# One chunk more of lead for the turned and rectified rows in the second and third mean pass of a graph kernel

## The chip, the cores and the metric

The kernel runs on one core of a Trainium2 chip. The metric is the device time of one execution in microseconds (us); lower is better. Three timed executions of the kernel before stand beside one profiled execution.

## The reference

The inputs are 50,000 nodes with 128 features (`x`), 25,000 edges (`src`, `dst`, sorted by `dst`) and edge features. Two layers follow each other; the change lies in the first.

```python
def _sage_conv(x, src, dst, Wl, bl, Wr):
    msg = x[src]
    summed = jax.ops.segment_sum(msg, dst, num_segments=N_NODES)
    mean = summed / jnp.maximum(cnt, 1.0)[:, None]
    return mean @ Wl.T + bl + x @ Wr.T
h = jax.nn.relu(_sage_conv(x, ...Wl0, bl0, Wr0))
h = jax.nn.relu(_sage_conv(h, ...Wl1, bl1, Wr1))
h = _sage_conv(h, ...Wl2, bl2, Wr2)
x = _layernorm(x + h)      # then an edge attention and a second layernorm
```

## The kernel before

Edges are cut into 49 chunks of 512 (NC), nodes into 98 (NN). There are three mean passes, `mean0`, `mean1` and `mean2`, one for each convolution. Each walks over the 49 edge chunks, computes the segment sums as a running scan that a flag resets, and writes mean times Wl to a table in HBM (`mean_product`). `mean1` and `mean2` read the table of the pass before them, so a pass can gather only when all stores of the pass before have landed. Beside their 49 edge chunks, `mean1` and `mean2` also carry half of the node chunks each through a "dense" chain, which is what a node without incoming edges needs.

One step of `mean1` or `mean2` works on several chunks at once. `run(engine, phase, stages, count)` writes for each engine its stages in a fixed order, each with a lead: in step s a stage with lead k treats chunk s+k. Engines agree through semaphores alone. Before the change, step s holds, in this order on each engine:

- TensorE (PE): `mean_prod` s+1 (L894, four products of the scanned sums with Wl), `mean_turn` s+3 (L883 turns the gathered rows GX into bank5, L887 adds hsrc times Wr), then the dense chain: `chain_t` s+9 (L771), `chain_1` s+8 and `chain_2` s+7 (both L849), `chain_y` s+6 (L869).
- ScalarE (ACT): `mean_keep` s+3 (L1062, relu of bank5 into `hsrc`), dense `keep_t` s+9 (L1026), `keep_1` s+8 (L1031), `keep_2` s+7 (L1036), `inverse_root` s+6 (L1047, L1050), `bias_y` s+8 (L1040).
- VectorE (DVE): `mean_seg` s+3 (L1385, the scan of hsrc into `seg`), `mean_scale` s+1 (L1392, into `prod`), dense `add_x` s+6 (L1339, then L1347 and L1352, the statistics), `norm` s+5 (L1363).
- SyncE's DMA queue: the flags of chunk s+6 (L564), the dense rows XN of s+13 (L551), the store of mean_product s+1 (L569) and the store of the dense result s+5 (L558).
- GpSimd (POOL): four indirect gathers of 128 rows for each chunk into GX (L672), and a copy of indices every four chunks (L662). GX has 8 buffers; the gather of chunk c waits until `mean_turn` of chunk c-8 is done.

`mean_turn` waits for its gathered rows and, since bank5 is the only bank for it, for `mean_keep` of the chunk before. `mean_keep` waits for `mean_turn` of its chunk, and writes to a place in `hsrc` of its own for each chunk. `mean_seg` waits for `mean_keep` of its chunk, for its flags and for the scan before. `inverse_root` waits for the statistics that VectorE makes in the same step.

Of the kernel before, what the change touches and what calls it, by code (L numbers as in the profile page):

```python
# [37 lines left out]
DENSE = 5  # L38
# [87 lines left out]
def run(eng, phase, stages, count, to_end=True, middle=None):  # L126

    stages = [(*one, count)[:3] for one in stages]  # L130
    whole = min(chunks - 1 - lead for lead, _, chunks in stages) // U

    def single(s):
        for lead, f, chunks in stages:
            if 0 <= s + lead < chunks:
                f(At(phase, (s + lead) // U, (s + lead) % U, to_end and s + lead == chunks - 1))

    for s in range(-max(lead for lead, _, _ in stages), 0):
        single(s)
    if middle:  # L140
        middle()
    with eng.Fori(0, whole) as j:
        for u in range(U):
            for lead, f, _ in stages:
                f(At(phase, j, u + lead))
    for s in range(whole * U, count):
        single(s)
# [15 lines left out]
def gnn_kernel(nc, x, src, dst, ea, Wl0, bl0, Wr0, Wl1, bl1, Wr1, Wl2, bl2, Wr2,  # L163
# [27 lines left out]
    with ExitStack() as ctx:  # L191
# [577 lines left out]
        def _(pe):  # L769
# [156 lines left out]
            for i in range(3):  # L926
                if i == 0:
                    run(pe, "mean0", [(LAG + 1, mean_turn), (0, look_up), (LAG, mean_prod)], NC, middle=table_sums)
                    look_done.end(pe, "mean0")
                    for one in (6, 7):  # L930
                        pe.matmul(bank[one][:, :], ident[:, :], hsrc[:, 0:CH], start=True, stop=True).then_inc(y_cleared, 1)
                else:
                    dense = first if i == 1 else second
                    run(pe, f"mean{i}", [(1, mean_prod), (3, mean_turn), (DENSE + 4, dense(chain_t)), (DENSE + 3, dense(chain_1)),
                                         (DENSE + 2, dense(chain_2)), (DENSE + 1, dense(chain_y))], NC)
                m_h.end(pe, f"mean{i}")
            m_scaled.end(pe, "mean2")
# [70 lines left out]
        def _(act):  # L1008
# [55 lines left out]
            for i in range(3):  # L1064
                if i:
                    m_seg.end(act, f"mean{i - 1}")
                if i == 0:
                    run(act, "mean0", [(0, mean_keep)], NC)
                    act.wait_ge(y_cleared, 2)
                    act.wait_ge(small_loaded, 16 * (H + 3))  # L1070
                else:
                    dense = first if i == 1 else second
                    run(act, f"mean{i}", [(3, mean_keep), (DENSE + 4, dense(keep_t)), (DENSE + 3, dense(keep_1)),
                                          (DENSE + 2, dense(keep_2)), (DENSE + 1, dense(inverse_root)), (DENSE + 3, dense(bias_y))], NC)
            run(act, "dst", [(4, keep_t), (3, keep_1), (2, keep_2), (1, inverse_root), (3, bias_y)], NC)
            y_done.end(act, "dst")
# [497 lines left out]
```

## Time and profile before

| what | value |
|---|---|
| median of 3 runs | 2632.78 us (2631.59 to 2633.68) |
| profiled execution, its own time | 2643.03 us |
| its span | 2641.2 us |
| PE, DVE, ACT, POOL busy over the span | 68%, 65%, 43%, 67% |
| `mean1`, first to last scan | 463.9 to 750.9 us |
| `mean2`, first to last scan | 780.3 to 1066.6 us |
| all DMA traffic of the program | 357.05 MB, mean 135 GB/s |

The two passes together are some 600 us of the 2641. Busy shares are averages over stages with different limits, so they do not tell what sets the pace in these two passes; the views of the passes do.

### The profile page before, as it was taken

How to read it: one execution, taken by the hardware profiler on the slowest of the kernel's cores; microseconds unless marked ns; L12 is line 12 of the kernel's file. 1: busy time of each engine (PE TensorE's matmuls, PEld its weight loads, DVE VectorE, ACT ScalarE, POOL GpSimd, SP SyncE). 2: the span in 40 equal slices, each digit the busy share in tenths (PEclk: the TensorE clock that was granted, in tenths of full speed). 3: DMA queues.
4: the chain of work that ended last, by engine and by line, in shares of the span. 5: the costliest groups of instructions: out<-in, count | busy, mean ns of one | idle time of the engine just before them, and what ended most of it. 6: DMA issues, size and time to landing. Idle time of an engine off the chain costs nothing.

```text
span 2641.2 us, 42521 instructions
## 1 busy us (share of the span) xinstructions
PE 1787.9 (68%) x9906; PEld 1270.0 (48%) x9906; DVE 1719.1 (65%) x5656; ACT 1142.2 (43%) x2655; POOL 1778.3 (67%) x1895
## 2 busy tenths in 40 slices
PE   4755667988879889676777663888788788770000
PEld 2335665656656656455555453555555555540000
DVE  7777886878767778565555533888788788871000
ACT  7951112545445545132222222776666666640000
POOL 0047775676657666467777777777777777776776
PEclk7558989999999999788888885999999999985555
DMA  0025666899989998544444613455545445433321
GB/s 20 1 65 145 166 158 137 187 175 187 182 173 184 202 176 182 152 139 122 129 134 133 171 59 106 145 158 155 145 139 151 144 147 153 148 95 106 93 92 51
DMA packets 366865, 357.05 MB, mean 135 GB/s; under 512 B 46547, under 2 KB 288862, under 8 KB 366722
## 3 DMA queue, kind: packets, MB, share of 16 engines
q1 hardware_dynamic: 310274, 246.46, 30.9%
q0 software_dynamic: 56448, 109.10, 22.9%
q14 instruction: 105, 0.86, 0.1%
q8 instruction: 38, 0.62, 0.1%
HBM read 232.89 MB, written 129.11 MB: 137 GB/s over the span
## 4 chain that ended last, share of the span: by engine, by line
POOL 23%; issue 21%; DVE 20%; PE 15%; DMA 9%; ACT 8%; DVEq 1%; SPq 1%; POOLq 1%; ACTq 0%
POOL hsrc L672 9%; POOL GX L672 8%; POOL out_dram L726 4%; DVE stats L1347 4%; PE bank L849 4%; DMA GX<-in_x_dram,idx_a 2%; PE bank L923 2%; PE bank L771 2%; PE bank L853 2%; ACT normed L1017 2%; DVE prod L1392 2%; DMA XN<-in_x_dram 2%; ACT hsrc L1062 2%; ACT normed L1018 2%; DVE res L1339 2%
## 5 line engine op out<-in xcount | busy, mean ns | idle before, releaser
L672 POOL DMA_INDIRECT GX<-mean_product,idx_a x392 | 416.2, 1062 | 125.4 <-issue 113.8
L672 POOL DMA_INDIRECT GX<-in_x_dram,idx_a x392 | 378.9, 967 | 117.8 <-issue 109.1
L849 PE MATMUL bank<-h,wt 128*128 128x512 f32 x588 | 328.2, 670 | 1.2 <-ACT h L1036 0.9
L1047 ACT ACTIVATE logv<-mv,eps 128x4 f32<-128x4 f32 x245 | 72.3, 295 | 518.7 <-DVE mv L1352 518.6
L726 POOL DMA_INDIRECT x_prime<-normed,idx_b x196 | 198.5, 1013 | 88.0 <-issue 81.7
L726 POOL DMA_INDIRECT out_dram<-XN,idx_b x196 | 193.1, 985 | 74.7 <-issue 63.4
L672 POOL DMA_INDIRECT hsrc<-x_prime,idx_d x196 | 190.3, 971 | 59.7 <-issue 59.7
L672 POOL DMA_INDIRECT GX<-in_edge_attr_dram,idx_a x196 | 189.3, 966 | 58.6 <-issue 54.1
L672 POOL DMA_INDIRECT hsrc<-x_prime,idx_c x196 | 186.3, 951 | 59.7 <-issue 59.7
L1385 DVE TENSOR_TENSOR_SCAN seg<-flag,seg,hsrc 128x512 f32<-128x512 bf16 x98 | 126.1, 1286 | 115.5 <-ACT hsrc L1062 73.4
L869 PEld LDWEIGHTS bank<-wt,h 128*128 128x128 f32 x1176 | 153.0, 194 | 49.8 <-issue 47.4
L771 PE MATMUL bank<-ident,XN 128*128 128x128 f32 x784 | 131.4, 294 | 65.8 <-DMA XN<-in_x_dram 27.4
L771 PE MATMUL bank<-ident,hsrc 128*128 128x128 f32 x468 | 86.5, 316 | 124.2 <-DMA hsrc<-x_prime,idx_d 67.3
L894 PE MATMUL bank<-wt,seg 128*128 128x128 f32 x1176 | 163.0, 283 | 7.2 <-DVE prod L1392 4.8
L1142 ACT ACTIVATE normed<-bank,shift,rstd 128x128 f32<-128x128 f32 x392 | 147.7, 457 | 45.4 <-DVE shift L1542 45.2
L771 PE MATMUL bank<-ident,GX 128*128 128x128 f32 x392 | 73.1, 318 | 133.6 <-DMA GX<-in_x_dram,idx_a 133.6
L1334 DVE TENSOR_TENSOR res<-bank,GX 128x512 f32<-128x512 f32 x49 | 33.9, 691 | 196.5 <-PE bank L869 196.3
L1363 DVE TENSOR_SCALAR normed<-res,mv,rstd 128x128 f32<-128x128 f32 x588 | 161.5, 352 | 0.0
L853 PEld LDWEIGHTS bank<-ident,hsrc 128*128 128x128 f32 x784 | 127.7, 231 | 68.3 <-issue 68.3
L771 PEld LDWEIGHTS bank<-ident,XN 128*128 128x128 f32 x784 | 100.6, 151 | 123.9 <-issue 120.3
L869 PE MATMUL bank<-wt,h 128*128 128x128 f32 x1176 | 157.2, 277 | 0.8 <-ACT h L1036 0.8
L894 PEld LDWEIGHTS bank<-wt,seg 128*128 128x128 f32 x1176 | 148.8, 198 | 13.5 <-DVE seg L1385 12.8
(222 smaller groups left out, 4584.2 us busy)
## 6 DMA issues: line engine op xcount, KB each, us to landing
mean_product<-prod SPq DMA_DIRECT2D x147, 256.0 KB, 4.0
hsrc<-mean_product SPq DMA_DIRECT2D x147, 256.0 KB, 4.3
XN<-in_x_dram SPq DMA_DIRECT2D x98, 256.0 KB, 6.4
x_prime<-normed SPq DMA_DIRECT2D x98, 256.0 KB
XN<-x_prime SPq DMA_DIRECT2D x98, 256.0 KB, 4.5
out_dram<-normed SPq DMA_DIRECT2D x98, 256.0 KB
flag<-same_dst_row SPq DMA_DIRECT2D x147, 128.0 KB, 5.5
XN<-low_row SPq DMA_DIRECT2D x98, 128.0 KB
```

The source lines that it names most:

```text
L672: pool.indirect_dma_start(buf[:, c.slot(U), t, :], None, table, bass.IndirectOffsetOnAxis(ap=idx[:, c.slot(U), t:t + 1], axis=0)).then_inc ...
L726: pool.indirect_dma_start(table, bass.IndirectOffsetOnAxis(ap=idx_b[:, c.slot(U), t:t + 1], axis=0), rows[:, t, :], None, bounds_check=N - ...
L771: return pe.transpose(dst, src, ident[0:src.shape[0], 0:src.shape[0]])
L849: last = pe.matmul(psum[:, :], wt[:, T_R[i], :], before[:, c.slot(2), :], start=True, stop=not dst_phase)
L853: last = pe.matmul(psum[:, t * P:(t + 1) * P], PL[:, c.slot(U), i, t, :], ident[:, :], start=False, stop=t == TPC - 1)
L869: last = pe.matmul(y[:, t * P:(t + 1) * P], h2[:, c.slot(2), t * P:(t + 1) * P], wt[:, T_R[2], :], start=False, stop=t == TPC - 1, skip_gr ...
L894: last = pe.matmul(bank[3 + c.slot(2)][:, t * P:(t + 1) * P], seg[:, c.slot(2), t * P:(t + 1) * P], wt[:, T_L[int(c.phase[-1])], :], start ...
L1047: act.activation(logv[:, s, :], mv[:, s, :, 1], ACT.Ln, bias=eps[:, 0:1]).then_inc(n_log.of(c), 1)
L1142: last = act.activation(normed[:, node.slot(4), t, :], norm_rows(node)[:, t, :], ACT.Identity, bias=shift[:, s, t:t + 1], scale=rstd[:, s, ...
L1347: last = dve.bn_stats(stats[:, s, t, :], rows[:, t, :])
L1363: last = dve.tensor_scalar(normed[:, c.slot(4), t, :], norm_rows(c)[:, t, :], mv[:, s, t, 0:1], rstd[:, s, t:t + 1], ALU.subtract, ALU.mult)
L1385: dve.tensor_tensor_scan(seg[:, c.slot(2), :], flag[:, c.slot(4), :], rows, seg[:, before.slot(2), CH - 1:CH], ALU.mult, ALU.add).then_inc ...
```

## The change

The stages `mean_turn` on TensorE and `mean_keep` on ScalarE get lead 4 in place of 3 in `mean1` and `mean2`. The scan on VectorE keeps lead 3. No instruction is added or removed.

```diff
@@ -931,7 +931,7 @@
                 else:
                     dense = first if i == 1 else second
-                    run(pe, f"mean{i}", [(1, mean_prod), (3, mean_turn), (DENSE + 4, dense(chain_t)), (DENSE + 3, dense(chain_1)),
+                    run(pe, f"mean{i}", [(1, mean_prod), (4, mean_turn), (DENSE + 4, dense(chain_t)), (DENSE + 3, dense(chain_1)),
                                          (DENSE + 2, dense(chain_2)), (DENSE + 1, dense(chain_y))], NC)
@@ -1070,7 +1070,7 @@
                 else:
                     dense = first if i == 1 else second
-                    run(act, f"mean{i}", [(3, mean_keep), (DENSE + 4, dense(keep_t)), (DENSE + 3, dense(keep_1)),
+                    run(act, f"mean{i}", [(4, mean_keep), (DENSE + 4, dense(keep_t)), (DENSE + 3, dense(keep_1)),
                                           (DENSE + 2, dense(keep_2)), (DENSE + 1, dense(inverse_root)), (DENSE + 3, dense(bias_y))], NC)
```

VectorE's order of instructions is the same before and after. On TensorE, this is the head of `mean1`, where the dense chain (L771, L849, L869) runs alone before the first turn:

```order
 L849 MATMUL bank<-h,wt 128x512 x2
 L869 MATMUL bank<-wt,h 128x128 x4
+L883 MATMUL bank<-ident,GX 128x128 x4
+L887 MATMUL bank<-hsrc,wt 128x512
 L771 MATMUL bank<-ident,XN 128x128 x4
 L849 MATMUL bank<-h,wt 128x512 x2
```

The first turn (L883, L887) now stands one step of the dense chain earlier. On ScalarE, this is the same place, where `keep` of the first chunk (L1062) moves ahead of one more step of the dense copies:

```order
 L1050 ACTIVATE rstd<-logv 128x4
 L1040 ACTIVATE bank<-b 128x512
+L1062 ACTIVATE hsrc<-bank,bcol 128x512
 L1026 ACTIVATE h<-bank 128x512
 L1031 ACTIVATE h<-bank,bcol 128x512
```

Every later L1062 then stands where the one of the chunk before stood, so inside the loop the rows read alike and only the chunk number differs. At the end of a pass on TensorE, after the dense chain has ended, one pair of turn and product rows falls away from between the products (L894):

```order
 L887 MATMUL bank<-hsrc,wt 128x512
-L894 MATMUL bank<-wt,seg 128x128 x4
-L883 MATMUL bank<-ident,GX 128x128 x4
-L887 MATMUL bank<-hsrc,wt 128x512
-L894 MATMUL bank<-wt,seg 128x128 x8
+L894 MATMUL bank<-wt,seg 128x128 x12
```

The last turn has moved ahead by one step, and the last three products stand together.

## Rows read from the trace of the kernel before

**Rows 1.** Waits, 460 to 745 us (mean1): us in total, times, longest us.
```profile
POOL idx_a L662 <- PE bank L887: 40.3, 6, 14.2
...
DVE seg L1385 <- ACT hsrc L1062: 35.4, 40, 1.1
...
PE bank L883 <- ACT hsrc L1062: 16.3, 35, 1.8
...
PE bank L771 <- DMA XN<-in_x_dram: 15.3, 5, 7.0
DVE seg L1385 <- DMA flag<-same_dst_row: 12.2, 4, 4.2
```
**Rows 2.** Waits, 780 to 1060 us (mean2), same columns.
```profile
PE bank L883 <- ACT hsrc L1062: 17.8, 35, 1.8
```
**Rows 3.** Chain that ended last, one step of mean1: start us, us, what.
```profile
510.33 0.67 DVE prod L1392
511.00 0.61 DVE res L1339
511.63 0.88 DVE stats L1347 x4
...
512.82 0.23 DVE mv L1352 x2
...
513.07 0.31 ACT logv L1047
...
514.03 0.68 ACT hsrc L1062
```
**Rows 4.** Timeline, DVE, scans: start us, us, engine line op, [idle before <-releaser].
```profile
509.13 1.28 DVE L1385 TENSOR_TENSOR_SCAN seg<-flag,seg,hsrc 128x512 f32<-128x512 bf16 x1 [1.02 <-ACT hsrc L1062]
...
555.87 1.28 DVE L1385 TENSOR_TENSOR_SCAN seg<-flag,seg,hsrc 128x512 f32<-128x512 bf16 x1 [1.01 <-ACT hsrc L1062]
...
740.59 1.28 DVE L1385 TENSOR_TENSOR_SCAN seg<-flag,seg,hsrc 128x512 f32<-128x512 bf16 x1 [0.18 <-ACT hsrc L1062]
...
745.67 1.28 DVE L1385 TENSOR_TENSOR_SCAN seg<-flag,seg,hsrc 128x512 f32<-128x512 bf16 x1 [0.18 <-ACT hsrc L1062]
```
**Rows 5.** Timeline, PE, head of mean1, same columns.
```profile
459.83 0.60 PE L883 MATMUL bank<-ident,GX 128*128 128x128 f32 x4
...
461.13 0.60 PE L771 MATMUL bank<-ident,XN 128*128 128x128 f32 x4
...
467.63 1.05 PE L869 MATMUL bank<-wt,h 128*128 128x128 f32 x8
...
472.87 1.05 PE L869 MATMUL bank<-wt,h 128*128 128x128 f32 x8
```
**Rows 6.** Source line L672, 600.3 to 646.5 us: ns min/median/max, first and last start.
```profile
L672 POOL DMA_INDIRECT GX<-mean_product,idx_a x32: 940/945/1870, 601.1 to 644.5; - x32
```
**Rows 7.** DMA, stretches 473-518, 518-570, 625-680, 870-945 us in turn.
```profile
XN<-in_x_dram SPq DMA_DIRECT2D x8, 256.0 KB, 3.9
...
q1 hardware_dynamic: 7835, 7.57, 43.5%
...
XN<-in_x_dram SPq DMA_DIRECT2D x8, 256.0 KB, 15.1
...
XN<-in_x_dram SPq DMA_DIRECT2D x8, 256.0 KB, 14.7
...
q1 hardware_dynamic: 12347, 11.76, 48.8%
```
**Rows 8.** Timeline, DVE, scans around the longest stall of mean1.
```profile
651.03 1.28 DVE L1385 TENSOR_TENSOR_SCAN seg<-flag,seg,hsrc 128x512 f32<-128x512 bf16 x1 [0.82 <-ACT hsrc L1062]
...
677.69 1.28 DVE L1385 TENSOR_TENSOR_SCAN seg<-flag,seg,hsrc 128x512 f32<-128x512 bf16 x1 [2.33 <-issue]
```
**Rows 9.** Source line L1385, 473.5 to 735.4 us, then 790 to 1050 us.
```profile
L1385 DVE TENSOR_TENSOR_SCAN seg<-flag,seg,hsrc x42: 1282/1284/1341, 473.8 to 729.9; 128x512 f32<-128x512 bf16 x42
...
L1385 DVE TENSOR_TENSOR_SCAN seg<-flag,seg,hsrc x42: 1282/1283/1337, 790.3 to 1044.5; 128x512 f32<-128x512 bf16 x42
```

## The prediction

> **What bounds the two passes now.** I read the waits of each pass first, then the chain that ended last, then the timeline of one step, and at last what the DMA queues did stretch by stretch. In the waits of mean1 the scan on VectorE waits 40 times for ScalarE's L1062, 35.4 us in all, and TensorE's turn waits for the same line 35 times, 16.3 us [rows 1]; mean2 has 17.8 us of the latter [rows 2]. The chain shows why: in a step it goes from VectorE's scale, add and statistics to ScalarE's logv, then to L1062, and from there into the scan of the same step [rows 3]. So VectorE waits for a copy that stands on ScalarE behind work that waits for VectorE itself. The pace of this ring is read from scans eight steps apart, 509.13 and 555.87: 5.84 us a step, with 1.0 us of VectorE's idle time ahead of the scan at each end [rows 4].
>
> The second thing that the reader is to see is that this is not the pace of a pass. From 473.8 to 729.9 lie 41 steps, 6.25 us each, and from 790.3 to 1044.5 as many, 6.20 us each [rows 9]. The 0.4 us between 5.84 and these, some 15 to 17 us a pass, is lost in clusters of long steps. One is between the scans at 651.03 and 677.69: three steps in 26.66 us, 9.1 us more than three of 5.84 [rows 8]. In the waits the names there are DMAs: XN on TensorE, 15.3 us in 5 waits up to 7.0, and flags on VectorE, 12.2 us in 4 [rows 1]. These loads are issued three or more steps ahead of use. The DMA views show them getting late gradually: XN lands after a median of 3.9 us in 473-518, 15.1 us in 518-570, and 14.7 in 625-680 [rows 7].
>
> **The change, part by part.** L883, L887 and L1062 of chunk c run one step earlier against everything else; nothing is added. After it, the scan of step s reads what ScalarE wrote in step s-1, so VectorE's wait of about 0.7 to 1.1 us goes. What is late next:
>
> - VectorE alone: the step from scan 740.59 to 745.67 takes 5.08 us with 0.18 us of idle time [rows 4], so 4.90 us of work.
> - TensorE alone: between two L869 in the head, where it never waits and has the turn, the dense chain and the product, lie 472.87 - 467.63 = 5.24 us [rows 5]. This is the next bound, 0.60 us below 5.84. That TensorE waits only 0.4 us a step now (16.3 us over some 40 steps, rows 1) says about the same.
> - GpSimd: 32 gathers (8 chunks) start between 601.1 and 644.5, 31 pitches of 1.40 us, thus 5.6 us a chunk without waiting for anybody [rows 6]. It waits now for 40.3 us in mean1 because it is up to 8 chunks ahead [rows 1]. With TensorE at 5.24, GpSimd uses up that lead and becomes the bound at 5.6, most of all in mean2, where its first gather has only just landed when the pass begins. The gain there is 0.24 us a step.
> - TensorE's turn still waits for L1062 of the chunk before. In both orders that L1062 stands in the step before, behind the same statistics, so that ring is as long as it was: VectorE's add to L1062's end (0.61+0.88+0.23+0.31+0.68 and the copies between, 514.71 - 511.00 = 3.7 us, rows 3) and then TensorE's turn to its L869, less than a step of 5.24. Below 9 us for two steps, it does not bind.
>
> In the head of a pass the first turn goes ahead of one more dense step. It costs what lies between L883 at 459.83 and L771 at 461.13, 1.30 us [rows 5], and TensorE is the bound there, so I count it in full: 2.6 us for two passes. At the end the same 1.30 us falls away, but VectorE sets the pace there, and I count nothing for it (at most 1 us a pass, its short waits before the last scans).
>
> Now the DMA. SyncE's queue moves 3 x 256 KB + 128 KB a step, 0.918 MB; at 5.84 us a step that is 157 GB/s. In 518-570 it moved 7.57 MB, 146 GB/s, while loads grew late; in 870-945 it moved 11.76 MB, 157 GB/s, what was asked [rows 7]. At 5.6 us a step 164 GB/s would be asked, at 5.24 us 175. So where loads are late already, the DMA's rate sets the time and the change gives nothing. Where they are not, it gives 0.24 to 0.60 us a step. The trace does not show a step without the ring, so I bound the sum from both sides. Above: all 84 steps gain 0.60 us, 50 us. Below: all are held by the DMA, 0 us, and a loss is treated as a rival. I take half of the steps, 42, as free of late loads (the starts of the passes, 870-945, and the ends, where the dense loads have stopped), and the middle of 0.24 and 0.60, 0.42 us: 17.6 us. Less 2.6 us in the heads this is 15 us.
>
> The Trainium skill's page "DMA: Bandwidth & Descriptors", section "Issuing engines are not separate DMA queues", says that DMAs of all issuing engines run on the same 16 DMA engines and interleave. The growth of the landing times while GpSimd gathers without a pause agrees with it; taken alone it would say that more requests in less time only queue, and the sum would be that of the first rival.
>
> Against the profiled execution's own time, 2643.03 us, that makes 2628. The median of the runs shown is 10.2 us below the profiled one, so the median to expect is 2632.78 - 15 = 2617.8, say 2618 us.
>
> **The rivals.**
>
> *The DMA gives all of it back.* Steps get shorter until the flags or XN are late, and the clusters grow by what the steps saved. For it: the mean of 6.2 us is worth 147 GB/s on SyncE's queue over a whole pass, as much as it reached in 518-570 with loads 15 us late. Against it: 157 GB/s in 870-945. The time: 0 to 5 us less, about 2630 us. Chance 0.20.
>
> *The whole ring's gain arrives.* DMA lateness is a matter of bursts, not of the rate, and the early rows give slack in the clusters too. All 84 steps gain 0.42 us, 35 us, less 2.6: 2600 us, and 2585 if GpSimd keeps up and it is 0.60. For it: TensorE and VectorE wait for L1062 in all undisturbed steps. Against it: GpSimd's 5.6 us and the late loads. Chance 0.15.
>
> *Slower: more clusters.* GX comes free a step earlier and steps are shorter, so GpSimd pauses less; its pauses (40.3 us in mean1, rows 1) are when SyncE's queue catches up. If both queues press all the time, another cluster of 9.1 us [rows 8] comes up again and again. The forecast's gross gain of 17.6 us, less the heads' 2.6, is eaten by 1.6 more clusters in all; from there it is a loss, and with three more it is 27.3 - 15 = 12 us, 2645 us. The page named above speaks for this too, beside the rows. Against it: bytes are the same, and a cluster ends by itself when GpSimd runs out of buffers. Chance 0.12.
>
> **How the numbers follow.** The forecast, a gain of 5 to 25 us, has 0.53; its own range is 2608 to 2628. A measurement of this kernel tells 0.2%, 5.3 us, from no change. Faster by more than that: the forecast and the second rival, 0.68. Within it: the first rival, 0.20. Slower: 0.12. The range takes in the first rival and most of the second (down to a gain of 37 us): 2596 to 2634 us; outside are the slower case and the extreme of the second, together about 0.15 to 0.2.
>
> **What the profile after would show.** The waits of DVE seg for ACT hsrc should nearly vanish from both passes (from 35.4 us to a few), and those of PE L883 for hsrc too. Undisturbed steps, eight scans apart, should fall from 5.84 to between 5.24 and 5.6 us. GpSimd's waits for PE L887 should shrink well below 40.3 us, and TensorE may wait for GX in mean2. Waits for XN and flags should stay or grow; the mean step should be near 6.0 us. I am wrong if undisturbed steps stay at 5.84 (then another ring binds, through TensorE's turn and L1062), if the DMA waits grow by as much as the steps shorten, or if they vanish with the ring.

## The result, and the profile after

The changed kernel is slower: a median of 2651.69 us (2641.38 to 2660.82, 9 runs) against 2634.31 us (2631.59 to 2644.13, 9 runs), ratio 1.0062 with a 95% interval of 1.0046 to 1.0079, some 16 us. Its profiled execution took 2651.59 us, 8.6 us more than that of before. From the first to the last scan mean1 takes 755.3 - 460.8 = 294.5 us (before 287.0) and mean2 1077.3 - 784.7 = 292.6 us (before 286.3): 14 us more in the two passes.

The waits of the changed kernel in 460 to 745 us (us in total, times, longest us):

```profile
POOL idx_a L662 <- PE bank L887: 48.0, 3, 21.7
DVE seg L1385 <- issue: 43.7, 7, 11.1
PE bank L771 <- DMA XN<-in_x_dram: 31.9, 7, 11.0
...
DVE seg L1385 <- DMA flag<-same_dst_row: 14.3, 3, 6.6
...
PE bank L883 <- ACT hsrc L1062: 3.3, 2, 2.5
```

The wait of the scan for ScalarE's L1062, 35.4 us in [rows 1], is gone from the list, and TensorE's wait for it fell from 16.3 to 3.3 us. So the change does what it says. But the waits for XN went from 15.3 to 31.9 us, and the scan now has 43.7 us of "issue" in 7 waits, where before it had 10.2 us in 2. "Issue" is idle time for which this view names no releaser; in the cluster at 522 to 565 us below, the chain that ended last has the flags' DMA there. GpSimd waits for TensorE a little longer than before (48.0 us for 40.3), in 3 pieces where there were 6.

The scans of the changed kernel, in the timeline, show both halves of the story:

```profile
511.38 1.28 DVE L1385 TENSOR_TENSOR_SCAN seg<-flag,seg,hsrc 128x512 f32<-128x512 bf16 x1
516.62 1.28 DVE L1385 TENSOR_TENSOR_SCAN seg<-flag,seg,hsrc 128x512 f32<-128x512 bf16 x1
521.97 1.28 DVE L1385 TENSOR_TENSOR_SCAN seg<-flag,seg,hsrc 128x512 f32<-128x512 bf16 x1
530.27 1.28 DVE L1385 TENSOR_TENSOR_SCAN seg<-flag,seg,hsrc 128x512 f32<-128x512 bf16 x1 [3.10 <-DMA flag<-same_dst_row]
541.67 1.28 DVE L1385 TENSOR_TENSOR_SCAN seg<-flag,seg,hsrc 128x512 f32<-128x512 bf16 x1 [6.51 <-issue]
555.43 1.28 DVE L1385 TENSOR_TENSOR_SCAN seg<-flag,seg,hsrc 128x512 f32<-128x512 bf16 x1 [8.85 <-issue]
```

Undisturbed steps take 5.24 us, TensorE's bound of [rows 5], in place of 5.84 [rows 4], with no idle time ahead of the scan. Then come steps of 8.3, 11.4 and 13.8 us, and the next scan is at 564.90, 9.5 us later. I call such a run of long steps a cluster. As a measure for all kernels below I take, over both passes, all steps above 6.1 us less 5.84 us each: 31 us before (4 clusters), 95 us in the changed kernel (5). So the clusters cost 64 us more, the other steps gain some 50 us, and the two passes lose 14 us.

The DMA view of the changed kernel in 480 to 500 us and then in 640 to 660 us (queue, packets, MB, share of 16 engines' time; then loads with their median time to landing) shows what happens in a cluster:

```profile
q0 software_dynamic: 446, 0.93, 50.9%
q1 hardware_dynamic: 3168, 2.99, 44.1%
...
XN<-in_x_dram SPq DMA_DIRECT2D x4, 256.0 KB, 5.9
...
q0 software_dynamic: 496, 1.02, 75.8%
q1 hardware_dynamic: 1452, 1.38, 20.9%
...
XN<-in_x_dram SPq DMA_DIRECT2D x2, 256.0 KB, 29.1
```

q0 is the queue of GpSimd's gathers, q1 that of SyncE. For almost the same bytes the gathers hold the engines for 75.8% of the time in place of 50.9%, and SyncE's queue falls from 150 to 69 GB/s. XN lands after 29 us and not 6. The kernel before, in 480 to 500 us, has a third value for the same bytes of gathers:

```profile
q1 hardware_dynamic: 3013, 2.96, 45.1%
q0 software_dynamic: 438, 0.91, 33.2%
```

The records of the single packets say where the time goes: a gather packet of 4096 bytes took 0.47 us on average in these 20 us of the kernel before, 0.71 and 0.97 us in the two stretches of the changed kernel, while a packet of SyncE's queue took 45 to 48 ns in all three.

A cluster ends soon after GpSimd stops gathering. The last gather before this pause starts at 552.75, and the scan of 564.90 is the last late one:

```profile
572.29 0.19 POOL L662 COPY idx_a<-lookup 128x16 int32 x1 [18.60 <-PE bank L887]
```

In all nine clusters of the two kernels such a pause of GpSimd (or the end of the pass's gathers) begins 2 to 11 us before the last late scan. It does not stop for want of a GX buffer, though. By the code the copy of the next four chunks' indices (L662) also waits for TensorE: ahead of the gather of chunk 23 it needs the turn of chunk 19, where the buffer needs only that of chunk 15. The gathers of chunks 0 to 22 had been started by 553.7, the scan of chunk 15 started at 555.43 (so its turn was done), and the copy came at 572.29, between the scans of chunks 17 and 18. At every fourth chunk GpSimd is therefore held to 4 chunks ahead of the turn, in both kernels.

The stretches 520-560 and 560-600 us of the changed kernel (PE, PEld, which is TensorE's loading of weights, DVE, ACT, POOL busy us, granted clock, DMA share, GB/s) show what TensorE has of it: it is busy for 26.24 of 40 us in the cluster with a granted clock of 0.85 on average, against 38.93 us and 0.98 behind it. They also show a DMA that is "busy" for 97% of the time at 138 GB/s, against 92% at 228:

```profile
520.00:560.00 40.00, 26.24 (x129) 17.51 (x129) 20.45 (x71) 13.68 (x31) 25.91 (x28) 0.85 0.97 138
560.00:600.00 40.00, 38.93 (x213) 26.97 (x213) 33.80 (x108) 23.93 (x52) 21.14 (x22) 0.98 0.92 228
```

### The profile page after: what moved, and what is told of

Its sections match the earlier page's. It is cut to its first block, busy times and chain, and to the rows that moved or that the text cites. A ratio compares the mean times of both kernels' runs of the same rounds, so it can differ in the third digit from the quotient of the medians.

```text
span 2649.8 us, 42529 instructions
## 1 busy us (share of the span) xinstructions
PE 1787.7 (67%) x9906; PEld 1272.2 (48%) x9906; DVE 1717.9 (65%) x5656; ACT 1143.3 (43%) x2655; POOL 1757.6 (66%) x1895
## 4 chain that ended last, share of the span: by engine, by line
POOL 24%; PE 23%; issue 18%; DVE 16%; DMA 10%; ACT 5%; SPq 4%; POOLq 1%; DVEq 0%; ACTq 0%
POOL GX L672 9%; POOL hsrc L672 8%; PE bank L849 7%; POOL out_dram L726 4%; DMA flag<-same_dst_row 3%; PE bank L771 3%; PE bank L869 3%; DMA GX<-in_x_dram,idx_a 2%; PE bank L894 2%; DVE stats L1347 2%; PE bank L853 2%; DMA XN<-in_x_dram 2%; ACT normed L1017 2%; PE bank L923 2%; ACT normed L1018 2%
## 5 line engine op out<-in xcount | busy, mean ns | idle before, releaser
L672 POOL DMA_INDIRECT GX<-mean_product,idx_a x392 | 393.3, 1003 | 121.6 <-issue 114.3
L672 POOL DMA_INDIRECT GX<-in_x_dram,idx_a x392 | 379.8, 969 | 117.8 <-issue 109.6
L849 PE MATMUL bank<-h,wt 128*128 128x512 f32 x588 | 336.1, 685 | 1.2 <-ACT h L1036 0.9
L672 POOL DMA_INDIRECT hsrc<-x_prime,idx_d x196 | 188.9, 964 | 59.7 <-issue 59.7
L672 POOL DMA_INDIRECT GX<-in_edge_attr_dram,idx_a x196 | 189.5, 967 | 58.5 <-issue 53.8
L672 POOL DMA_INDIRECT hsrc<-x_prime,idx_c x196 | 186.2, 950 | 59.7 <-issue 59.7
L771 PE MATMUL bank<-ident,XN 128*128 128x128 f32 x784 | 132.5, 296 | 99.1 <-DMA XN<-in_x_dram 62.7
L1385 DVE TENSOR_TENSOR_SCAN seg<-flag,seg,hsrc 128x512 f32<-128x512 bf16 x98 | 125.5, 1280 | 112.0 <-issue 70.0
L869 PEld LDWEIGHTS bank<-wt,h 128*128 128x128 f32 x1176 | 153.8, 195 | 51.9 <-issue 50.8
L771 PEld LDWEIGHTS bank<-ident,XN 128*128 128x128 f32 x784 | 101.0, 152 | 158.8 <-issue 155.7
L894 PE MATMUL bank<-wt,seg 128*128 128x128 f32 x1176 | 163.7, 284 | 10.4 <-DVE prod L1392 7.1
L771 PE MATMUL bank<-ident,hsrc 128*128 128x128 f32 x468 | 87.1, 318 | 116.0 <-DMA hsrc<-x_prime,idx_d 55.1
L771 PE MATMUL bank<-ident,GX 128*128 128x128 f32 x392 | 72.9, 317 | 132.2 <-DMA GX<-in_x_dram,idx_a 132.2
L853 PEld LDWEIGHTS bank<-ident,hsrc 128*128 128x128 f32 x784 | 127.9, 231 | 69.4 <-issue 69.4
L869 PE MATMUL bank<-wt,h 128*128 128x128 f32 x1176 | 157.2, 277 | 0.8 <-ACT h L1036 0.8
L894 PEld LDWEIGHTS bank<-wt,seg 128*128 128x128 f32 x1176 | 150.1, 200 | 15.4 <-DVE seg L1385 13.5
```

The costliest lines, as they stand in the source:

```text
L672: pool.indirect_dma_start(buf[:, c.slot(U), t, :], None, table, bass.IndirectOffsetOnAxis(ap=idx[:, c.slot(U), t:t + 1], axis=0)).then_inc ...
L771: return pe.transpose(dst, src, ident[0:src.shape[0], 0:src.shape[0]])
L849: last = pe.matmul(psum[:, :], wt[:, T_R[i], :], before[:, c.slot(2), :], start=True, stop=not dst_phase)
L853: last = pe.matmul(psum[:, t * P:(t + 1) * P], PL[:, c.slot(U), i, t, :], ident[:, :], start=False, stop=t == TPC - 1)
L869: last = pe.matmul(y[:, t * P:(t + 1) * P], h2[:, c.slot(2), t * P:(t + 1) * P], wt[:, T_R[2], :], start=False, stop=t == TPC - 1, skip_gr ...
L894: last = pe.matmul(bank[3 + c.slot(2)][:, t * P:(t + 1) * P], seg[:, c.slot(2), t * P:(t + 1) * P], wt[:, T_L[int(c.phase[-1])], :], start ...
```

## The experiments

Ratios are against the kernel before, run on the same chip. Each profile is one execution, so the cluster figures of single kernels are rough; ratios rest on several runs. The first four kernels ask how far GpSimd's reach and the pace matter.

**e1_lead4_gx4**, the changed kernel with GpSimd at most 4 chunks ahead:

```diff
-                pool.wait_ge(m_turned.of(c), m_turned.after(c, U))
+                pool.wait_ge(m_turned.of(c), m_turned.after(c, U if c.phase == "mean0" else 4))
```

> The changed kernel with one more limit: in the second and third mean pass the gather of a chunk waits for the turn of the chunk 4 before it, not 8 before it, so GpSimd runs at most 4 chunks ahead. Theory D (the DMA engines are shared, and once SyncE's loads are late, unpaused gathers keep them late until GpSimd runs out of buffers): clusters end after half as many gathers and cost about half; they cost 46 us in each pass of the changed kernel (steps above 6 us, over 5.24 each), so 20 to 40 us less in all, 2612 to 2632 us. Rival O (the new order itself is at fault: TensorE's turn ahead of the dense chain, clock drops on TensorE): no change, 2645 to 2655 us. Rival G (GpSimd's reach of 8 chunks is needed, so less of it makes TensorE wait for gathered rows): slower than the changed kernel, over 2660 us.

Measured: 2639.7 us, ratio 0.9993 (0.9972 to 1.0015). By the ratios some 18 us are gone, and with them the loss, but the expectation failed: the time lies in none of the three ranges, and the clusters, which were to cost half, still sum to 86 us over 5.84 where they were 95, in more and shorter pieces. GpSimd's waits in 460 to 745 us are now on the gathers:

```profile
POOL GX L672 <- PE bank L887: 25.1, 5, 9.8
...
POOL idx_a L662 <- PE bank L887: 4.2, 2, 2.9
```

The longest pause is 9.8 us in place of 21.7. The copy of the indices held GpSimd to 4 chunks at every fourth chunk already, so this limit adds less than "4 in place of 8" says. Rival G is out at 4 chunks, and rival O as it was put (no change) too.

**e2_lead4_paced**, useless work on VectorE ahead of each scaled product:

```diff
+                if c.phase != "mean0":
+                    dve.tensor_tensor(pad[:, c.slot(2), 0:TPC, :], by_tile(bank[3 + c.slot(2)][:, :]), inv, ALU.mult)
+                    dve.tensor_tensor(pad[:, c.slot(2), TPC:TPC + 2, :], by_tile(bank[3 + c.slot(2)][:, :])[:, 0:2, :], inv[:, 0:2, :], ALU.mult)
```

> The changed kernel with about 1.0 us of useless work on VectorE in each step of the two passes: the scaled product is computed twice more, one and a half times in all, into a scratch tensor. Nothing is left out. A step is then bound by VectorE at about 4.85 + 1.0 = 5.85 us, the pace of before, in the new order. Theory D: the queue is asked for 157 GB/s as before, the clusters shrink to those of the kernel before, and the time goes back to 2630 to 2640 us although work is added. Rival O: the loss of the order stays and the added work comes on top where VectorE is late, 2655 to 2680 us.

Measured: 2655.31 us, ratio 1.0068 (1.0045 to 1.0092). Steps are 5.75 us and the clusters shrink from 95 to 44 us, so 0.5 us a step of added work cost nothing against the changed kernel. But the time did not go back to that of before: the clusters are still above 31 us, and the added work lengthens the ends of the passes by some 3 us each. The expectation failed in its number, which is the lowest that rival O allowed, and this run alone does not settle pace against order.

**e3_before_gx4**, the kernel before with the same edit as e1:

> The kernel before with GpSimd at most 4 chunks ahead in the two passes. Theory D: the two clusters of each pass (15.6 and 13.7 us over steps of 5.86) shrink by half or go, 10 to 25 us less, 2610 to 2625 us. Rival G: TensorE waits for gathered rows, slower than 2640 us. If reach does not matter to the clusters: 2630 to 2638 us.

Measured: 2633.06 us, ratio 0.9969 (0.9949 to 0.9990); clusters 24 us. It is the only kernel here that leaves nothing out and beats both, by 0.3%. That is less than theory D expected; the time lies in the range given for "reach does not matter", and only the ratio, whose interval stays below 1, speaks against that.

**e4_lead4_mean1_only**, `(4 if i == 1 else 3, mean_turn)` on TensorE and the same for `mean_keep` on ScalarE:

> The change in the second mean pass (mean1) alone; the third has lead 3 as before. Every theory that works pass by pass, D and O alike, expects about half of the loss of 16 us: 2639 to 2646 us, with mean1 as in the changed kernel (first to last scan 294 us) and the third pass as before (286 us). If the loss comes from how the second pass hands over to the third, it is all here or not at all.

Measured: 2646.75 us, ratio 1.0025 (0.9998 to 1.0052), some 40% of the loss. The interval takes in 1, so the time alone would not settle it. Its profile does: mean1 takes 291.2 us from first to last scan, with clusters of 46 us over 5.84, and the third pass 285.8 us with 14 us, as before. The loss is made pass by pass.

The next four take load off the DMA, and go on with the reach.

**e5_before_light_loads** and **e6_lead4_light_loads**:

```diff
+                n = TPC if isinstance(c.j, int) and c.index() < U else 1
-                sp.dma_start(XN[:, c.slot(U), :, :], file_rows(x, N, c)).then_inc(x_in.of(c), 16)
+                sp.dma_start(XN[:, c.slot(U), 0:n, :], file_rows(x, N, c)[:, 0:n, :]).then_inc(x_in.of(c), 16)
```

> The kernel before, in which the loads of dense rows (XN) fetch only 64 of 256 KB from the ninth chunk of each pass on; the rest of XN keeps rows of earlier chunks, so that part of the layer norm's result is that of other nodes. SyncE's queue is asked for 0.72 MB a step in place of 0.92, 123 GB/s at 5.84 us. Theory D: loads are no longer late, the clusters (13.7 to 15.6 us a pass) go, 20 to 32 us less than before: 2600 to 2615 us. If the clusters do not come from the load on the DMA: 2630 us or more.

> The changed kernel with the same light loads (the same part left out): 137 GB/s at 5.24 us a step, below the 146 GB/s at which loads grew late. Theory D: with the clusters gone the ring's gain arrives, steps of 5.24 to 5.6 us, 20 to 45 us less than the kernel before with light loads: 2560 to 2590 us. Rival O (the order costs by itself): not faster than the kernel before with light loads.

Measured: 2606.24 us, ratio 0.9888 (0.9851 to 0.9925), for the kernel before: no step above 6.1 us is left, and a pass takes 270 us. The clusters of before do come from the load on the DMA. But the changed kernel with light loads took 2620.36 us, ratio 0.9948 (0.9923 to 0.9974): slower than the kernel before with light loads, with clusters of 71 us. Its waits in 470 to 740 us still have XN and flags:

```profile
DVE seg L1386 <- issue: 22.6, 5, 6.7
PE bank L772 <- DMA XN<-in_x_dram: 18.2, 8, 4.4
DVE seg L1386 <- DMA flag<-same_dst_row: 14.6, 3, 6.1
```

It asks SyncE's queue for only 137 GB/s, so my limit of 146 GB/s was wrong. The expectation of 2560 to 2590 us failed, and what rival O had said held.

**e7_lead4_gx2** and **e8_before_gx2**, the edit of e1 with 2 in place of 4:

> The changed kernel with GpSimd at most 2 chunks ahead of TensorE's turn in the two passes. Theory D: a cluster can hold 2 chunks of gathers in place of 4, so it is shorter again: 5 to 20 us below the changed kernel with 4 (whose ratio to before was 0.999), 2612 to 2632 us. Rival G: four gathers take 5.0 us and land 3 us later, so 2 chunks are just enough for steps of 5.24; if they are not, TensorE waits for GX by 0.5 us or more a step, over 2660 us.

> The kernel before with GpSimd at most 2 chunks ahead. Theory D: the clusters shrink further than with 4 chunks (ratio 0.997): ratio 0.990 to 0.996, 2608 to 2624 us. Rival G: TensorE waits for GX, ratio above 1.

Measured: 2638.5 us, ratio 1.0008 (0.9986 to 1.0030), and 2647.91 us, ratio 1.0042 (1.0019 to 1.0066). Both times lie above what theory D expected. For the changed kernel 2 chunks are as good as 4; for the kernel before they are worse than 8. The waits say that something else is late now. Those of e7 in 460 to 745 us have neither XN nor flags, which were 31.9 and 14.3 us in the changed kernel, and TensorE waits for gathered rows instead; its DMA view in 480 to 500 us has the gathers' share at its lowest:

```profile
PE bank L883 <- DMA GX<-mean_product,idx_a: 32.7, 27, 3.3
...
q0 software_dynamic: 460, 0.96, 22.4%
```

e8 has no waits for XN or flags there either, and 37.4 us for GX. So with 2 chunks SyncE's loads are no longer late in either kernel, and the gathers have become the bound. Half of e7's steps are above 5.7 us, and its 50 us over 5.84 are spread over 33 steps, where the changed kernel's 95 us lie in 21. In e8 steps stay at 5.8 us, and the last two of each pass take 5.5 to 7.7 us where they took 2.4 to 3.6. Rival G named this wait (0.7 us a step in e7), but not the time.

Next, pace against order, and the queue.

**e9_lead4_paced_light**, the edits of e2 and e6 together:

> The changed kernel with both edits: 1.0 us of useless work on VectorE in each step, and loads of dense rows cut to 64 of 256 KB (the rest of XN keeps other nodes' rows). It has the order of the changed kernel and the pace and DMA load of the kernel before with light loads, which had no cluster at all (0.9888 of before). Theory P (the pace is what tips the DMA into clusters): no cluster here either; steps of 5.74 us, ratio 0.985 to 0.993. Rival O (the order, with turns and gathers one chunk further ahead): clusters of 30 us a pass as in the changed kernel with light loads, ratio 0.997 to 1.01.

Measured: 2616.86 us, ratio 0.9902 (0.9868 to 0.9937). There is one cluster of 13 us in one pass, against the expectation, and none in the other, where e6 has 71 us with the same loads and order at 5.24 us.

**e10_scan_last**, the kernel before with VectorE's stages in another order:

```diff
-                    run(dve, f"mean{i}", [(3, mean_seg), (1, mean_scale), (DENSE + 1, dense(add_x)), (DENSE, dense(norm))], NC)
+                    run(dve, f"mean{i}", [(1, mean_scale), (DENSE + 1, dense(add_x)), (DENSE, dense(norm)), (3, mean_seg)], NC)
```

> The kernel before, TensorE, ScalarE and GpSimd as they were (lead 3), but the scan stands last in VectorE's step and not first. It then reads a chunk that ScalarE wrote 4 us earlier, so the ring is broken as by the change, in the order of before on the other engines. Theory P: steps fall to about 5.24 us, clusters of 45 us a pass appear as in the changed kernel, ratio 1.003 to 1.010. Rival O: steps fall to 5.24 and clusters stay as before, ratio 0.980 to 0.992.

Measured: 2651.54 us, ratio 1.0039 (1.0020 to 1.0058). With lead 3 everywhere, steps fall to 5.24 us and clusters of 79 us appear. Scans of it in the timeline, undisturbed and at the start of a cluster:

```profile
533.70 1.27 DVE L1385 TENSOR_TENSOR_SCAN seg<-flag,seg,hsrc 128x512 f32<-128x512 bf16 x1
538.92 1.28 DVE L1385 TENSOR_TENSOR_SCAN seg<-flag,seg,hsrc 128x512 f32<-128x512 bf16 x1
549.86 1.27 DVE L1385 TENSOR_TENSOR_SCAN seg<-flag,seg,hsrc 128x512 f32<-128x512 bf16 x1
```

So the pace makes clusters, whichever edit makes the pace: slower at one order (e9 against e6), nearly all of them go; faster at the other order (e10), they come. Rival O as it was put for e9 and e10 falls. A small part for the order is not ruled out: at 5.75 us a step the changed order has 44 us of clusters for 31 (e2 against the kernel before) and 13 for 0 (e9 against e5), one profile each and with steps 0.1 us shorter.

**e11_lead4_loads_on_act** and **e12_before_loads_on_act**: `flag_load` and `x_load` leave SyncE's stages of the two passes and stand at the end of ScalarE's.

```diff
-            run(sp, "mean1", [(6, flag_load), (DENSE + 8, first(x_load)), (1, prod_store), (DENSE, first(x_store))], NC)
+            run(sp, "mean1", [(1, prod_store), (DENSE, first(x_store))], NC)
...
-                                          (DENSE + 2, dense(keep_2)), (DENSE + 1, dense(inverse_root)), (DENSE + 3, dense(bias_y))], NC)
+                                          (DENSE + 2, dense(keep_2)), (DENSE + 1, dense(inverse_root)), (DENSE + 3, dense(bias_y)),
+                                          (6, act_flag_load), (DENSE + 8, dense(act_x_load))], NC)
```

> The changed kernel with the loads of flags and dense rows of the two passes issued by ScalarE, at the end of its step, so that they travel in a queue of their own beside the stores (SyncE) and the gathers (GpSimd). Same bytes. Theory Q (within theory D: in a cluster SyncE's one queue gets one turn for each turn of the gathers, and loads wait behind stores): loads keep landing in 5 to 10 us, clusters shrink, ratio 0.975 to 0.995. If the 16 engines are simply full, nothing changes: ratio 1.003 to 1.010. ScalarE has room for two issues of about 0.4 us a step (3.9 of 5.24 us are busy).

> The kernel before with the same move of loads to ScalarE's queue. ScalarE is in the ring here, so two issues of 0.4 us at the end of its step, between the statistics and the next L1062, lengthen each step by up to 0.8 us: 84 steps, up to 67 us slower. Theory Q: less the clusters' 30 us; ratio 1.00 to 1.015.

Measured: 2660.87 us, ratio 1.0078 (1.0055 to 1.0100), and 2662.0 us, ratio 1.0075 (1.0051 to 1.0099). Theory Q falls. In a cluster of e11, 520 to 560 us, the DMA view reads:

```profile
q0 software_dynamic: 936, 1.92, 67.8%
q10 hardware_dynamic: 1635, 2.25, 18.0%
q1 hardware_dynamic: 2530, 1.97, 14.6%
...
XN<-in_x_dram ACTq DMA_DIRECT2D x4, 256.0 KB, 18.5
```

q10 is ScalarE's queue. The two together have 32.6% where the gathers have 67.8%; in the same 40 us of the changed kernel SyncE's queue alone has 27.3% and the gathers 69.4%. The loads land about as late as there (XN 18.5 us for 19.6). TensorE waits less for XN over the pass, but the stores are late in their place: VectorE waits 32.4 us in 470 to 750 us for mean_product's stores. What is short lies behind both queues. The Trainium skill's page "DMA: Bandwidth & Descriptors", section "Issuing engines are not separate DMA queues", says that DMAs of all issuing engines run on the same 16 DMA engines and interleave. This run agrees: the three shares sum to 100%.

e12 has steps of 6.3 to 6.9 us, which fits ScalarE's issues standing in the ring, and in 470 to 740 us no wait for XN or flags at all (mean2 has three steps of 7.3 to 8.4 us): a third sign that the pace decides.

By then the cause of the failed forecast was open in one point: what part of the traffic tips it at 5.24 us.

**e13_lead4_2kb_rows** and **e14_before_2kb_rows**, with `near_rows` for the stores and loads of the mean tables, and five VectorE instructions that map the indices once:

```diff
+            return take(table, c.index() * CH, CH).rearrange("(q t) d -> q t d", t=TPC)
...
-                sp.dma_start(sorted_rows(prod_table[int(c.phase[-1])], c), prod[:, c.slot(4), :, :]).then_inc(m_stored.of(c), 16)
+                sp.dma_start(near_rows(prod_table[int(c.phase[-1])], c), prod[:, c.slot(4), :, :]).then_inc(m_stored.of(c), 16)
```

> The changed kernel with another layout of the mean tables in HBM: row q*4+t of a chunk in place of t*128+q, so that each store of mean_product is 128 pieces of 2 KB in place of 512 of 512 bytes (and so each load of it in the next phase). Same bytes; the indices are mapped once on VectorE, so the result is the reference's. SyncE's queue then moves 512 pieces a step in place of 896. Theory N (the number of pieces a us, 171 at 5.24 us a step against 153 at 5.84, tips the DMA engines, not the bytes): clusters mostly go at 5.24 us a step too, and with them 60 to 95 us; ratio 0.970 to 0.985. If bytes and the held engines count alone: clusters as in the changed kernel, ratio 1.003 to 1.010.

> The kernel before (lead 3) with the same layout. Theory N: its clusters go, 25 to 31 us, ratio 0.987 to 0.991, and slower than the changed kernel with this layout by 84 x 0.3 to 0.5 us. Otherwise 0.997 to 1.003.

Measured: 2655.8 us, ratio 1.0068 (1.0046 to 1.0089), and 2645.26 us, ratio 1.0027 (1.0007 to 1.0047). Theory N falls: the number of SyncE's pieces is not it. The one profile of e13 is of its fastest execution (2635.63 us), and even that has 84 us of clusters; e14 has 52. Against the same kernels with 512-byte rows, the kernel before lost 0.3% by 2 KB rows, and the changed one nothing that is clear of noise (1.0068 for 1.0062).

**e17_lead4_half_gathers** and **e18_before_half_gathers**:

```diff
-                for t in range(TPC):
+                half = c.phase in ("mean1", "mean2")
+                for t in range(2 if half else TPC):
...
-bass.IndirectOffsetOnAxis(ap=idx[:, c.slot(U), t:t + 1], axis=0)).then_inc(sig.of(c), 16)
+bass.IndirectOffsetOnAxis(ap=idx[:, c.slot(U), t:t + 1], axis=0)).then_inc(sig.of(c), 32 if half else 16)
```

> The changed kernel with two of four gathers for each chunk left out in the two passes (the other half of GX keeps rows of the first pass). SyncE's queue carries all of its bytes, 175 GB/s asked at 5.24 us a step; GpSimd asks 25 GB/s in place of 50. Theory H (in a cluster the engines are held by the gathers, whose share went from 51 to 76% for the same bytes, and SyncE's queue gets the rest): no clusters at 5.24 us a step, and the ring's gain is seen with SyncE's full load: passes of 49 scans in 245 to 255 us, 60 to 80 us less in all, ratio 0.970 to 0.978. If SyncE's 175 GB/s alone are too much: clusters stay, ratio above 0.990.

> The kernel before with the same half of the gathers left out. Theory H: no clusters, steps of 5.84, passes of 270 us as with light loads, ratio 0.987 to 0.990. The difference to the changed kernel with half gathers is the ring's gain without the DMA's limit, 84 x 0.5 to 0.6 = 42 to 50 us less 3 us in the heads.

Measured: 2554.75 us, ratio 0.9661 (0.9640 to 0.9683), and 2613.12 us, ratio 0.9884 (0.9864 to 0.9904). e17 is faster than expected, e18 in its range. Neither has a step above 6.1 us. The changed kernel's passes take 242.4 us each, those of before 270.2 and 271.2. The DMA view of e17 in 480 to 700 us:

```profile
q1 hardware_dynamic: 40045, 37.28, 56.0%
q0 software_dynamic: 2561, 5.25, 23.1%
...
XN<-in_x_dram SPq DMA_DIRECT2D x35, 256.0 KB, 3.9
```

SyncE's queue carries 37.28 MB in 220 us, 169 GB/s, with loads landing after 3.9 us. So SyncE's full traffic at 5.24 us a step is no problem by itself. With the gathers halved, the ring's removal is worth 2613.12 - 2554.75 = 58 us, more than the 42 to 50 that I had worked out for 84 steps; the two passes have 96.

| kernel | step, us | clusters over 5.84, us | ratio |
|---|---|---|---|
| before | 5.84 | 31 | 1 |
| changed | 5.24 | 95 | 1.0062 |
| before, light loads (e5) | 5.84 | 0 | 0.9888 |
| changed, light loads (e6) | 5.24 | 71 | 0.9948 |
| changed, light loads, paced (e9) | 5.75 | 13 | 0.9902 |
| before, scan last (e10) | 5.24 | 79 | 1.0039 |
| before, half gathers (e18) | 5.84 | 0 | 0.9884 |
| changed, half gathers (e17) | 5.24 | 0 | 0.9661 |

## Why the prediction was wrong, point by point

- **The ring and its removal** were right. The scan's 35.4 us of waits for L1062 left the list, and undisturbed steps fell to the 5.24 us that I read between two L869. I sized its gain at 0.42 us for 42 steps, holding GpSimd's 5.6 us a chunk for the next bound. With half of the gathers it is 58 us; the passes are 27.8 and 28.8 us shorter, 0.6 us for each of 96 steps, which is the upper of my two values for a step. My lower one came from a wrong reading of [rows 6]. Of the 32 gathers there the median takes 945 ns and the longest 1870, and the timeline has six of 1.41 to 1.87 us, not more than one to a chunk, so what I had measured was not GpSimd's own pace. In the changed kernel the pitch of undisturbed gathers is 1.32 us, 5.3 us a chunk (31 from 479.5 to 519.1), and two gathers that nothing delays stand 1.25 us apart. Between clusters the changed kernel ran at 5.24 us, and at 4.8 us behind them, so GpSimd did not bind.
- **The step that failed** is this one: "So where loads are late already, the DMA's rate sets the time and the change gives nothing." It took the DMA's rate as given, and so the least gain as zero. In a cluster the rate is not given: the gathers hold the engines for longer for the same bytes, and SyncE's queue falls to 69 GB/s, half of the 146 GB/s that I took for late loads. A faster pace between clusters is paid back with more than it gained: clusters went from 31 to 95 us, and the other steps gained some 50 us. One of the prediction's own signs of being wrong, DMA waits that grow by as much as the steps shorten, is what came.
- **The limit in GB/s** (146 late, 157 not) was wrong as a rule. e6 asks for 137 GB/s of SyncE's queue and has clusters, e17 carries 169 GB/s and has none. What differs between the two is the gathers beside it, whole in e6 and halved in e17.
- **The slower rival**, with 0.12, came nearest: the loss is time in clusters. But by its reason GpSimd would pause less, and it paused for 48.0 us where it had paused for 40.3. Its price was off too: I gave a cluster 9.1 us [rows 8] and needed several more of them. Their number rose only from 4 to 5, but their length more: the one at 522 to 565 us costs 42.93 - 4 x 5.84 = 19.6 us, and the next, three steps of 11.74, 15.97 and 13.00, 23.2 us. Why they are longer is not shown. GpSimd does not lose its lead between them, as the prediction had it: counted at the scans, it has started the gathers of 4 chunks beyond the scanned one when a cluster of the changed kernel begins (3 at one of them), 3.75 in the kernel before, and the count stands still in undisturbed steps. Within a cluster it climbs to between 6.75 and 7.75 in the four long ones of the changed kernel, and to 4.5 to 5.0 in the kernel before. It goes on for longer before it pauses, and a reach of 2 chunks ends the late loads; but a reach of 4 shortened the clusters only from 95 to 86 us.
- **GpSimd's waits** were forecast "well below 40.3 us". They were 48.0 us. In mean1 of either kernel the long ones are one at the head and one in each of the first two clusters: 14.2, 9.4 and 13.1 us before, 7.7, 18.6 and 21.7 us after. They come with the clusters, and between them there is no long one.
- **The head of a pass** shows no cost. The first scan came at 460.8 us, 3.1 us earlier, but among the kernels with lead 3 it differs by more than that from profile to profile (460.7 in e8, 467.6 in e3). From the last scan of mean1 to the first of mean2 it is 29.4 us in both kernels, and the first two steps of a pass take 4.3 us in place of 5.0. The prediction's term of 2.6 us is not to be seen in the rows.
- **What stays open** is why gathers hold the engines for longer in a cluster, and whether halving them helps through their traffic or through GpSimd's pauses, which e17 has in plenty (108 us in 470 to 740 us). No run changes the wait of the index copy (L662), at which GpSimd stops in a cluster. That the same state comes at a faster pace, and not at a slower one with the same loads, is shown; what tips it is not.

## What to carry to other kernels

Where waits for DMAs come in clusters in the profile before, a shorter step elsewhere is not free of them: price the loss, not only the gain that is withheld, by asking which queue's work goes on while the others wait. Here it is GpSimd, whose gathers go on until a semaphore stops it; read in the code which one that is. A limit on how far they run ahead is a cheap thing to try: 4 chunks took back the changed kernel's loss (0.9993 for 1.0062), and 2 ended the late loads in both kernels but made everybody wait for the gathers. Before a ring between two engines is broken, run the kernel with the second limit taken away at either pace: it tells in one pair of runs what the ring is worth and what the second limit takes.

## What was not expected of the hardware

The share of time for which the DMA engines are "busy" says little about what they move: 97% at 138 GB/s in 520-560 us and 92% at 228 GB/s in 560-600 us of the changed kernel. For 0.91 to 1.02 MB in 20 us the gathers' queue held the engines for 22.4% (e7), 33.2% (before), 50.9% and, in a cluster, 75.8% of the time (changed kernel). A second issuing queue brought little more for the loads and stores together: 32.6% in e11, 27.3% in the same 40 us of the changed kernel. And storing rows in pieces of 2 KB in place of 512 bytes did not help (ratios 1.0027 and 1.0068).
